# The last F tile of each expert's first product, computed over two halves of 256 slots

## The chip, the cores and the metric

The kernel runs on one core of one Trainium2 chip. The metric is the device time of one execution in microseconds (us), the median of several runs. Three runs of the kernel before gave 821.24, 821.36 and 821.48 us. Less is better.

## The reference

A batch of 4 sequences of 1024 tokens (4096 tokens of width D = 512) passes through two layers, and the input is added at the end:

```
h     = x @ W_cond[category of the sequence] + b_cond[...]         # per sequence
probs = softmax(h @ Wr)                                            # 8 experts
e, p  = argmax(probs), max(probs)
# each expert takes the first 512 tokens that chose it (capacity 4096 / 8)
a     = relu(h[tokens of e] @ W1[e])                               # 512 -> F = 2048
y     = a @ W2[e]                                                  # 2048 -> 512
out   = x;  out[tokens of e] += p * y
```

Everything is float32. The two products of the experts are nearly all of the arithmetic: for each of 8 experts 512 x 512 x 2048 and 512 x 2048 x 512.

## The kernel before

**Three products for one.** Each float32 operand is split into a high part and a low part, both of type fp32r, and a product is the sum of three: high by high, high by low, low by high. `PARTS` on TensorE lists these three pairs. A product over K = 512 is cut in `DK` = 4 blocks of 128, so one output tile of 128 x 512 takes 4 x 3 = 12 matmuls that accumulate in one PSUM bank. Each matmul loads its own 128 x 128 weights first (PEld LDWEIGHTS in the profile), then streams 512 columns through them.

**Stages.** First the conditioned rows h of all 4096 tokens are computed (L968, L972, L984), with the router beside them (L890, L897, L910, L920, L928, L929, L939), and h is stored in DRAM. Then the tokens of the first expert are gathered and transposed (L1036, L1046, L1054). From then on a loop of 4 rounds of two experts each (`par` 0 and 1) does all expert work on TensorE.

**One expert on TensorE.** The first product is made in `FT` = 16 tiles (`j`) of 128 of the F = 2048 hidden units, each over all `CH` = 512 slots of the expert. The weights are a 128 x 128 block of W1, and the moving operand is the transposed tokens `xts`, 512 columns. Tiles 0 and 1 are made by `first_two` (L1092, in an order that follows the arrival of the token blocks), tiles 2 to 15 by the plain loop at L1123 (matmuls at L1133). The tiles go round `AR` = 4 PSUM banks `ffn_ps` (two halves of `acc_ps`, two of `tp_ps`); tile 15 is in the fourth, in `tp_ps`. The second product is made by `second(q)` (L1071, matmuls at L1080) for each quarter q of F: 4 slot blocks x 4 hidden tiles x 3 = 48 matmuls of 512 columns into `y_ps`. Quarter q - 1 follows the last tile of quarter q, so the order at the end of an expert is: tiles 12, 13, 14, 15, then `second(2)` with 48 matmuls, then `second(3)` with 48, then the first two tiles of the next expert. TensorE executes this order as written.

**What follows a tile.** The last matmul of a tile raises `s_acc`. ScalarE then applies Relu and writes the high part into `hts` (L592), VectorE computes the low part (L843) and raises `s_accf`, which frees the bank and lets `second` read the tile: `second(q)` waits for tile 4q + 3 (L1075). Behind each of these two steps the same engines split a piece of the next weights: ScalarE at L525 (W1) or L531 (W2), VectorE at L734 or L740. SyncE loads weights into `stage` (L257, L262), and GpSimd gathers and scatters rows (L421, L428, L460, L467). VectorE scales the outputs at L867.

The waits ahead of tile j at L1127 (weights split), L1129 and L1130 (bank free, that is, tile j - 4 has been read by ScalarE and VectorE) stand in front of its first matmul; the tile's one signal stands on its last.

Of the kernel before, what the change touches and what calls it, by code (L numbers as in the profile page):

```python
# [17 lines left out]
def moe_kernel(nc, x, x_t, cat, cond_w, cond_wt, cond_b, cond_br, w_r, w_1, w_2, out, h_rows):  # L18
# [6 lines left out]
    P = 128  # L25
# [6 lines left out]
    DK = D // P  # L32
    CH = 512
# [5 lines left out]
    FT = F // P  # L39
# [3 lines left out]
    HI, LO = 0, 1  # L43
# [13 lines left out]
    SPLIT_X = [None, None, (3, 4), (6, 7), (12, 14), (16, 17), (21, 22), (22, 24)]  # L57
    SPLIT_W = [None, (4, 4, 5, 5), (11, 11, 12, 13), (16, 17, 18, 19)]
    KEEP_FIRST = 12
    LATE = 4  # L60
    EARLY = TOKENS - LATE * P
    BY_TILE = NT - 2 * TPC
# [11 lines left out]
    with ctx:  # L74
        def sb(name, shape, dt):
            return ctx.enter_context(nc.sbuf_tensor(name, shape, dt))
# [9 lines left out]
        w1s = [sb(f"w1_split{n}", [P, 2, DK, CH], f32r) for n in (1, 0)][::-1]  # L86
        w2s = sb("w2_split", [P, 2, 2, DK, CH], f32r)
        with nc.sbuf_tensor("xt_first", [P, 2, DK, CH], f32), \
                nc.sbuf_tensor("late_parts", [P, 3, LATE, D], bf16) as late_parts:
            pass  # L90
        xts = sb("xt_split", [P, 4, 2, DK, CH], f32r)
# [45 lines left out]
        tok_all = sb("tok_all", [P, E, SB], u32)  # L137
        late_rel = sb("late_rel", [P, LATE], f32)
        window = sb("window", [P, LATE], f32)
        window_at = sb("window_at", [1, LATE], mybir.dt.int32)  # L140
        late_sel = sb("late_sel", [P, LATE, P], bf16)
        put_all = sb("put_all", [P, E, SB], u32)
# [11 lines left out]
        ffn_ps = [acc_ps[:, 0, :], acc_ps[:, 1, :], tp_ps[:, 0, :], tp_ps[:, 1, :]]  # L154
        AR = len(ffn_ps)
# [715 lines left out]
        def _(pe):  # L871
            PARTS = ((HI, HI), (HI, LO), (LO, HI))
# [126 lines left out]
            def keep_warm(times):  # L999

                for _ in range(times):
                    nc.tensor.matmul(acc_ps[:, 1, :], ones[:, :], zeros[:, :], start=True, stop=True)

            pe.wait_ge(s_mask, 1)
            pe.wait_ge(s_zeros, 1)
            keep_warm(KEEP_FIRST)
            pe.wait_ge(s_whalf, 1)
# [61 lines left out]
            with pe.Fori(0, E // 2) as pair:  # L1069
                for par in range(2):  # L1070
                    def second(q):  # L1071
                        pe.wait_ge(s_w2lo, pair * (4 * QN) + 2 * (par * QN + q + 1))
                        if q == 0:
                            pe.wait_ge(s_y, pair * (2 * SB) + par * SB + 1)
                        pe.wait_ge(s_accf, NT + pair * (2 * FT) + par * FT + QF * (q + 1))  # L1075
                        for s in range(SB):
                            for jj in range(QF):
                                j = q * QF + jj
                                for a, w in PARTS:
                                    last = nc.tensor.matmul(y_ps[:, s, :], hts[:, j % HB, a, s * P:(s + 1) * P],  # L1080
                                                            w2s[:, q % 2, w, jj, :],
                                                            start=(j == 0 and (a, w) == (HI, HI)),
                                                            stop=(j == FT - 1 and (a, w) == (LO, HI)))
                            if q == QN - 1:
                                last.then_inc(s_f2, 1)

                    def first_two():

                        x_of = pair * (2 * DK) + par * DK

                        def product(j, k, w, a, start=False, stop=False):
                            return nc.tensor.matmul(ffn_ps[j], w1s[0][:, w, k, j * P:(j + 1) * P],  # L1092
                                                    xts[:, par, a, k, :], start=start, stop=stop)

                        def with_high(k):
                            pe.wait_ge(s_xehi, x_of + k + 1)
                            product(0, k, HI, HI, start=(k == 0))
                            product(0, k, LO, HI)

                        def with_low(k):  # L1100
                            pe.wait_ge(s_xelo, x_of + k + 1)
                            return product(0, k, HI, LO, stop=(k == DK - 1))

                        pe.wait_ge(s_w1lo, pair * (4 * QN) + 2 * par * QN + 2)
                        pe.wait_ge(s_accf, NT + pair * (2 * FT) + par * FT + 2 - AR)
                        with_high(0)
                        product(1, 0, HI, HI, start=True)
                        with_high(1)
                        with_low(0)
                        with_high(2)  # L1110
                        with_low(1)
                        with_high(3)
                        with_low(2)
                        product(1, 0, LO, HI)
                        with_low(3).then_inc(s_acc, 1)
                        product(1, 0, HI, LO)
                        for k in range(1, DK):
                            for w, a in PARTS:
                                last = product(1, k, w, a, stop=(k == DK - 1 and (w, a) == (LO, HI)))
                        last.then_inc(s_acc, 1)  # L1120

                    first_two()
                    for j in range(2, FT):  # L1123
                        slot, jj = (j // QF) % 2, j % QF
                        tile = pair * (2 * FT) + par * FT + j
                        if jj == 0:
                            pe.wait_ge(s_w1lo, pair * (4 * QN) + 2 * (par * QN + j // QF + 1))  # L1127
                        if j == 2 and par == 0:
                            pe.wait_ge(s_quart, 1)  # L1129
                        pe.wait_ge(s_accf, NT + tile + 1 - AR)  # L1130
                        for k in range(DK):
                            for w, a in PARTS:
                                last = nc.tensor.matmul(ffn_ps[j % AR], w1s[slot][:, w, k, jj * P:(jj + 1) * P],  # L1133
                                                        xts[:, par, a, k, :],
                                                        start=(k == 0 and (w, a) == (HI, HI)),
                                                        stop=(k == DK - 1 and (w, a) == (LO, HI)))
                        last.then_inc(s_acc, 1)
                        if jj == QF - 1 and j // QF >= 1:
                            second(j // QF - 1)
                    second(QN - 1)  # L1140
# [34 lines left out]
```

## Time and profile before

| | |
|---|---|
| median of 3 runs | 821.36 us (821.24 to 821.48) |
| span of the profiled execution, first to last instruction | 819.6 us |
| PE busy | 812.9 us, 99%, 4103 matmuls |
| PEld busy | 668.0 us, 82%, 4103 weight loads |
| DVE, ACT, POOL busy | 410.4, 257.3, 241.2 us (50%, 31%, 29%) |
| mean granted TensorE clock | 1.000 |

The profile gives the profiled execution's own time as its span alone. The median of the runs is 1.76 us above that span. PE and PEld are two rows of the same engine: the matmuls, and the loading of their weights, which can run beside a matmul. A matmul's own duration is a latency from start to modelled end, so matmuls that follow each other overlap in the list; the time that one costs in a row of many is the step from one start to the next, which a row with a count gives: (busy - duration of one) / (count - 1), or busy / count in a chain.

### The profile page before, as it was taken

How to read it: one execution, taken by the hardware profiler on the slowest of the kernel's cores; microseconds unless marked ns; L12 is line 12 of the kernel's file. 1: busy time of each engine (PE TensorE's matmuls, PEld its weight loads, DVE VectorE, ACT ScalarE, POOL GpSimd, SP SyncE). 2: the span in 40 equal slices, each digit the busy share in tenths (PEclk: the TensorE clock that was granted, in tenths of full speed). 3: DMA queues.
4: the chain of work that ended last, by engine and by line, in shares of the span. 5: the costliest groups of instructions: out<-in, count | busy, mean ns of one | idle time of the engine just before them, and what ended most of it. 6: DMA issues, size and time to landing. Idle time of an engine off the chain costs nothing.

```text
span 819.6 us, 10809 instructions
## 1 busy us (share of the span) xinstructions
PE 812.9 (99%) x4103; PEld 668.0 (82%) x4103; DVE 410.4 (50%) x575; ACT 257.3 (31%) x350; POOL 241.2 (29%) x240
## 2 busy tenths in 40 slices
PE   9999999999999999999999999999999999999997
PEld 6778788888888888888888888888888888888886
DVE  5678877442644355533653174426443555336531
ACT  3322245330433133332433053304331333324330
POOL 1000127264304540273007320643045401030201
PEclk9999999999999999999999999999999999999999
DMA  8988454543443337341633344444533372216101
GB/s 286 362 293 289 186 174 150 211 141 142 155 179 128 129 103 256 115 139 58 211 122 126 142 154 154 141 141 159 174 128 128 98 256 102 102 59 210 50 0 51
DMA packets 61098, 127.14 MB, mean 155 GB/s; under 512 B 8310, under 2 KB 8310, under 8 KB 60562
## 3 DMA queue, kind: packets, MB, share of 16 engines
q1 hardware_dynamic: 47714, 95.19, 32.6%
q0 software_dynamic: 13216, 31.38, 11.8%
q8 instruction: 14, 0.23, 0.1%
q10 hardware_dynamic: 144, 0.26, 0.1%
q14 instruction: 10, 0.08, 0.0%
HBM read 110.13 MB, written 25.17 MB: 165 GB/s over the span
## 4 chain that ended last, share of the span: by engine, by line
PE 97%; DMA 1%; DVE 0%; SPq 0%; issue 0%; ACT 0%; POOL 0%; POOLq 0%
PE y_ps L1080 42%; PE tp_ps L1133 21%; PE acc_ps L1133 16%; PE acc_ps L984 6%; PE acc_ps L1092 5%; PE tp_ps L984 3%; DMA stage<-x_t 1%; PE tp_ps L910 1%; PE y_ps L890 0%; PE y_ps L939 0%; DVE xt_split L619 0%; PE y_ps L1036 0%; PE y_ps L1054 0%; SPq L281 0%; PE y_ps L920 0%
## 5 line engine op out<-in xcount | busy, mean ns | idle before, releaser
L1080 PE MATMUL y_ps<-w_split,xt_split 128*128 128x512 f32 x1536 | 352.1, 389 | 0.0
L1080 PEld LDWEIGHTS y_ps<-w_split,xt_split 128*128 128x128 f32 x1536 | 288.3, 188 | 59.9
L428 POOL DMA_INDIRECT rows<-h_rows,idx_all x112 | 117.2, 1047 | 240.3 <-DVE turned L833 198.8
L1133 PE MATMUL tp_ps<-xt_split,w_split 128*128 128x512 f32 x768 | 179.3, 389 | 0.0
L1133 PEld LDWEIGHTS tp_ps<-xt_split,w_split 128*128 128x128 f32 x768 | 144.2, 188 | 29.9
L592 ACT ACTIVATE xt_split<-acc_ps 128x512 fp32r<-128x512 f32 x64 | 38.3, 598 | 333.7 <-PE acc_ps L1092 171.6
L1133 PE MATMUL acc_ps<-xt_split,w_split 128*128 128x512 f32 x576 | 134.5, 389 | 0.0
L1133 PEld LDWEIGHTS acc_ps<-xt_split,w_split 128*128 128x128 f32 x576 | 108.1, 188 | 22.5
L843 DVE SCALAR_TENSOR_TENSOR xt_split<-acc_ps,xt_split 128x512 fp32r<-128x512 f32 x64 | 44.3, 692 | 162.7 <-ACT xt_split L592 161.8
L867 DVE SCALAR_TENSOR_TENSOR rows<-y_ps,p_cur,rows 128x512 f32<-128x512 f32 x32 | 24.0, 751 | 133.0 <-PE y_ps L1080 133.0
L734 DVE TENSOR_TENSOR w_split<-stage,w_split 128x1024 fp32r<-128x1024 f32 x66 | 81.0, 1227 | 16.3 <-ACT w_split L525 16.3
L740 DVE TENSOR_TENSOR w_split<-stage,w_split 128x1024 fp32r<-128x1024 f32 x64 | 78.5, 1227 | 16.4 <-ACT w_split L531 16.4
L467 POOL DMA_INDIRECT out<-rows,put_all x32 | 31.4, 981 | 154.3 <-DVE rows L867 154.3
L525 ACT ACTIVATE w_split<-stage 128x1024 fp32r<-128x1024 f32 x66 | 69.4, 1052 | 0.0
L531 ACT ACTIVATE w_split<-stage 128x1024 fp32r<-128x1024 f32 x64 | 67.3, 1052 | 0.0
L592 ACT ACTIVATE xt_split<-tp_ps 128x512 fp32r<-128x512 f32 x64 | 38.3, 598 | 75.1 <-PE tp_ps L1133 75.1
L843 DVE SCALAR_TENSOR_TENSOR xt_split<-tp_ps,xt_split 128x512 fp32r<-128x512 f32 x64 | 44.3, 692 | 34.9 <-ACT xt_split L592 34.9
L984 PE MATMUL acc_ps<-w_split,xt_split 128*128 128x512 f32 x228 | 55.1, 394 | 0.4 <-DVE rows L648 0.4
L421 POOL DMA_INDIRECT rows<-x,tok_all x32 | 44.9, 1403 | 31.3 <-DMA out<-rows,put_all 18.3
L984 PEld LDWEIGHTS acc_ps<-w_split,xt_split 128*128 128x128 f32 x228 | 42.2, 188 | 9.6 <-issue 1.1
L460 POOL DMA_INDIRECT out<-b_rows,drop_all x32 | 32.8, 1024 | 52.9 <-DMA b_rows<-x 43.7
L1092 PE MATMUL acc_ps<-xt_split,w_split 128*128 128x512 f32 x192 | 45.0, 390 | 0.1
(140 smaller groups left out, 381.9 us busy)
## 6 DMA issues: line engine op xcount, KB each, us to landing
stage<-w SPq DMA_DIRECT2D x64, 1024.0 KB, 6.5
b_rows<-x SPq DMA_DIRECT2D x8, 1024.0 KB, 7.7
h_rows<-rows POOLq DMA_DIRECT2D x6, 1024.0 KB, 9.8
stage<-cond_wt SPq DMA_DIRECT2D x4, 1024.0 KB, 9.8
x_more<-x_t SPq DMA_DIRECT2D x4, 1024.0 KB, 9.5
stage<-x_t SPq DMA_DIRECT2D x3, 1024.0 KB, 8.0
stage<-cond_w SPq DMA_DIRECT2D x3, 1024.0 KB, 9.6
h_rows<-rows SPq DMA_DIRECT2D x8, 256.0 KB, 2.5
```

Of the source, the lines that this page charges most:

```text
L421: pool.indirect_dma_start(out=rows[:, 1, s, :], out_offset=None, in_=x, in_offset=bass.IndirectOffsetOnAxis(ap=tok_all[:, e, s:s + 1], axi ...
L428: pool.indirect_dma_start(out=h_quart[:, t * P:(t + 1) * P], out_offset=None, in_=h_parts, in_offset=bass.IndirectOffsetOnAxis(ap=idx_all[ ...
L525: nc.scalar.activation(w1s[slot][:, HI, ks, :], stage[:, slot, ks, :], ACTF.Copy).then_inc(s_w1hi, 1)
L531: nc.scalar.activation(w2s[:, slot, HI, ks, :], stage[:, 2 + slot, ks, :], ACTF.Copy).then_inc(s_w2hi, 1)
L592: nc.scalar.activation(hts[:, j % HB, HI, :], ffn_ps[j % AR], ACTF.Relu).then_inc(s_hhi, 1)
L734: nc.vector.tensor_tensor(w1s[slot][:, LO, ks, :], stage[:, slot, ks, :], w1s[slot][:, HI, ks, :].bitcast(f32), ALU.subtract).then_inc(s_w ...
L740: nc.vector.tensor_tensor(w2s[:, slot, LO, ks, :], stage[:, 2 + slot, ks, :], w2s[:, slot, HI, ks, :].bitcast(f32), ALU.subtract).then_inc ...
L843: nc.vector.scalar_tensor_tensor(hts[:, j % HB, LO, :], ffn_ps[j % AR], 0.0, hts[:, j % HB, HI, :].bitcast(f32), ALU.max, ALU.subtract).th ...
L984: last = nc.tensor.matmul(cond_bank(n), xts[:, c % 4, a, k, t * P:(t + 1) * P], w2s[:, (c // CPB) % 2, w, k, :], start=(k == 0 and (a, w) ...
L1080: last = nc.tensor.matmul(y_ps[:, s, :], hts[:, j % HB, a, s * P:(s + 1) * P], w2s[:, q % 2, w, jj, :], start=(j == 0 and (a, w) == (HI, HI)),
L1092: return nc.tensor.matmul(ffn_ps[j], w1s[0][:, w, k, j * P:(j + 1) * P], xts[:, par, a, k, :], start=start, stop=stop)
L1133: last = nc.tensor.matmul(ffn_ps[j % AR], w1s[slot][:, w, k, jj * P:(jj + 1) * P], xts[:, par, a, k, :], start=(k == 0 and (w, a) == (HI, ...
```

## The change

The last of the 16 tiles of the first product, j = `FT` - 1 = 15, is computed in two passes: the 12 matmuls over slots 0 to 255, then the 12 over slots 256 to 511. Each pass goes through the same 12 blocks of weights, so each block is loaded twice, and each matmul streams 256 columns in place of 512. Both passes write halves of the same PSUM bank. The signal `s_acc` stands on the last matmul of the second pass, the waits ahead of the tile and all other engines' code are as before. Tiles 0 to 14 and the second product are unchanged.

```diff
+    HALVES = (slice(0, CH // 2), slice(CH // 2, CH))
...
                         pe.wait_ge(s_accf, NT + tile + 1 - AR)
-                        for k in range(DK):
-                            for w, a in PARTS:
-                                last = nc.tensor.matmul(ffn_ps[j % AR], w1s[slot][:, w, k, jj * P:(jj + 1) * P],
-                                                        xts[:, par, a, k, :],
-                                                        start=(k == 0 and (w, a) == (HI, HI)),
-                                                        stop=(k == DK - 1 and (w, a) == (LO, HI)))
+                        for cols in HALVES if j == FT - 1 else (slice(0, CH),):
+                            for k in range(DK):
+                                for w, a in PARTS:
+                                    last = nc.tensor.matmul(ffn_ps[j % AR][:, cols],
+                                                            w1s[slot][:, w, k, jj * P:(jj + 1) * P],
+                                                            xts[:, par, a, k, cols],
+                                                            start=(k == 0 and (w, a) == (HI, HI)),
+                                                            stop=(k == DK - 1 and (w, a) == (LO, HI)))
                         last.then_inc(s_acc, 1)
```

## Rows read from the trace of the kernel before

**Rows 1.** The page: span; busy us, share and count of each engine; granted clock in tenths.
```profile
span 819.6 us, 10809 instructions
PE 812.9 (99%) x4103; PEld 668.0 (82%) x4103; DVE 410.4 (50%) x575; ACT 257.3 (31%) x350; POOL 241.2 (29%) x240
...
PEclk9999999999999999999999999999999999999999
```
**Rows 2.** The page: the chain that ended last, share by engine and by line.
```profile
PE 97%; DMA 1%; DVE 0%; SPq 0%; issue 0%; ACT 0%; POOL 0%; POOLq 0%
PE y_ps L1080 42%; PE tp_ps L1133 21%; PE acc_ps L1133 16%; PE acc_ps L984 6%; PE acc_ps L1092 5%; PE tp_ps L984 3%; DMA stage<-x_t 1%; PE tp_ps L910 1%; PE y_ps L890 0%; PE y_ps L939 0%; DVE xt_split L619 0%; PE y_ps L1036 0%; PE y_ps L1054 0%; SPq L281 0%; PE y_ps L920 0%
```
**Rows 3.** The chain in order of time, first expert: start us, us, piece, count.
```profile
172.99 5.44 PE acc_ps L1133 x24
178.43 5.44 PE tp_ps L1133 x24
183.87 21.76 PE y_ps L1080 x96
205.63 5.44 PE acc_ps L1092 x24
```
**Rows 4.** Stretches of about one expert: us, busy us (count) by engine, PEclk, DMA share, GB/s.
```profile
206.00:293.00 87.00, 87.00 (x386) 72.03 (x385) 40.23 (x46) 27.26 (x36) 30.24 (x28) 1.00 0.42 145
...
728.00:815.00 87.00, 86.91 (x384) 71.63 (x382) 40.21 (x46) 27.27 (x36) 14.34 (x12) 1.00 0.21 75
```
**Rows 5.** Timeline at the end of the first expert: start us, us, engine, line, count.
```profile
183.71 12.63 PE L1080 MATMUL y_ps<-w_split,xt_split 128*128 128x512 f32 x55
...
183.91 0.60 ACT L592 ACTIVATE xt_split<-tp_ps 128x512 fp32r<-128x512 f32 x1 [1.17 <-PE tp_ps L1133]
...
184.54 0.69 DVE L843 SCALAR_TENSOR_TENSOR xt_split<-tp_ps,xt_split 128x512 fp32r<-128x512 f32 x1 [0.55 <-ACT xt_split L592]
```
**Rows 6.** Groups of the page: line, shapes, count, busy us, mean ns, idle before.
```profile
L1133 PE MATMUL tp_ps<-xt_split,w_split 128*128 128x512 f32 x768 | 179.3, 389 | 0.0
L1133 PEld LDWEIGHTS tp_ps<-xt_split,w_split 128*128 128x128 f32 x768 | 144.2, 188 | 29.9
```
**Rows 7.** Timeline of PE, f32 transposes of 128 columns, two overlapping windows.
```profile
114.55 1.06 PE L1054 MATMUL y_ps<-ident,x_more 128*128 128x128 f32 x7
114.55 1.18 PE L1054 MATMUL y_ps<-ident,x_more 128*128 128x128 f32 x8
```
**Rows 8.** Timeline of PE, f32 with 32-column weights, two overlapping windows and stretches.
```profile
45.79 1.95 PE L910 MATMUL tp_ps<-x_more,m 128*32 128x128 f32 x64
45.79 1.85 PE L910 MATMUL tp_ps<-x_more,m 128*32 128x128 f32 x60
```
**Rows 9.** Timeline of PE, bf16 matmuls of 128 columns.
```profile
113.18 1.31 PE L1036 MATMUL y_ps<-late_sel,late_parts 128*128 128x128 bf16 x20
```
**Rows 10.** Timeline of the weight loads (PEld) in the first stage, around a pause.
```profile
6.69 0.19 PEld L968 LDWEIGHTS tp_ps<-w_split,xt_split 128*128 128x128 f32 x1
6.92 0.19 PEld L968 LDWEIGHTS y_ps<-w_split,xt_split 128*128 128x128 f32 x1
...
9.50 0.30 PEld L968 LDWEIGHTS acc_ps<-w_split,xt_split 128*128 128x128 f32 x2 [0.58 <-issue]
```
**Rows 11.** Timeline of the matmuls (PE) over the same stretch.
```profile
6.92 0.39 PE L968 MATMUL tp_ps<-w_split,xt_split 128*128 128x512 f32 x1
7.14 0.39 PE L968 MATMUL y_ps<-w_split,xt_split 128*128 128x512 f32 x1
...
9.53 0.70 PE L968 MATMUL acc_ps<-w_split,xt_split 128*128 128x512 f32 x2 [0.18 <-ACT w_split L499]
10.07 0.39 PE L968 MATMUL tp_ps<-w_split,xt_split 128*128 128x512 f32 x1
```
**Rows 12.** The page: DMA queues that carry instructions: packets, MB, share.
```profile
q8 instruction: 14, 0.23, 0.1%
...
q14 instruction: 10, 0.08, 0.0%
```

## The prediction

> **What bounds the kernel now.** I read the page first. TensorE's matmuls fill 812.9 of 819.6 us, every slice of the span shows nine tenths or more of the clock, and no other engine is over 50% busy [rows 1]. The chain that ended last is TensorE for 97%, with one hundredth for the first load of x; L1080, L1133 and L1092, the expert loop, make 84% [rows 2]. Then I read the chain in order of time. Its pieces in the expert loop have no gap: 24 matmuls take 5.44 us and 96 take 21.76 us, 226.7 ns each, one piece starting where the last ends [rows 3]. The table by stages says the same for each later expert: PE busy for 87.00 of 87.00 us and 384 to 386 matmuls, at a granted clock of 1.00 [rows 4]. So TensorE never waits from its first expert to its last, and a matmul added there, or a nanosecond added to one, is paid in full. Nor is there an idle moment for the change to win back.
>
> **What the change does not touch.** Its signal stands on the tile's last matmul, as before, so ScalarE and VectorE get the whole tile at once, and only as much later as the tile takes longer. What they do with it has room. Tile 15 ends at 183.87; Relu starts at 183.91 and the low part ends at 184.54 + 0.69 = 185.23 [rows 3, 5]. The first reader, the second half of the 96 matmuls, starts after 48 of them, at 183.87 + 10.88 = 194.75 [rows 3]. That is 9.5 us of room. A tile that is later by a fraction of a us moves these two engines, and the weight splits behind them, by the same fraction while TensorE is late by it too. So ScalarE, VectorE, SyncE's weight loads, GpSimd's gathers and every wait are worth 0, and what hides them is the 10.88 us of the third quarter's second product. That is also why nothing can be won by an earlier start: nobody waits for this tile. If the cover were gone, the tile's 1.3 us of Relu and low part would stand on the path, 8 times 1.3 = 10 us; nothing in the change takes it away. One wait stands ahead of tile 15, for the bank (L1130), and the matmuls run past it without a gap [rows 3]; the change adds none.
>
> **What it costs, step by step.** Removed: 12 matmuls of 512 columns per expert, 12 x 226.7 = 2720 ns. Added: 24 of 256 columns, each with its own weight load of the same size. The trace has no fp32r matmul of 256 columns, so its step s must be bounded. The break-even is 2720 / 24 = 113.3 ns; each ns of s over it costs 24 x 8 = 192 ns.
>
> Term one, the stream. In 226.7 ns at the full 2.4 GHz level, 512 columns take 213.3 ns at one column per clock, which leaves 13.3 ns beside them. Half the columns take 106.7 ns. If the 13.3 ns are paid once per matmul whatever its length, s = 120.0. The nearest row with weights of 128 columns in f32, the transposes of 128 columns, has one more matmul for 0.12 us (1.18 less 1.06) [rows 7]. Those are shorter than 256 columns and take as long, so they don't run at a column per clock; plain f32 with weights of 32 columns shows 0.10 us for four more that run side by side [rows 8], which is 128 columns at half pace. Their 0.12 us is then 106.7 + 13 to 15: a stretch of streaming as long as the new one, and about the same extra. The bf16 matmuls of 128 columns step by (1.31 - 0.22) / 19 = 57 ns [rows 9], 53.3 and a little. They show that pairs of load and matmul can be issued at least twice as fast as needed, so issue costs 0.
>
> Term two, the weight load. Its length of 188 ns [rows 6] is longer than 120, and is the reason to look closely. But it is a latency. After a pause two loads come together: two take 0.30 us, so the second starts 0.30 - 0.19 = 0.11 us after the first [rows 10]. One load thus holds its path for 0.11 us. And a load starts with the matmul ahead of it: the load for y_ps at 6.92, where the matmul for tp_ps starts at 6.92, and the matmul for y_ps at 7.14 [rows 10, 11]. So a load of about 110 ns lies beside a stream of 120 ns and is hidden, by 10 ns only. Today it is hidden by over 100. When it isn't hidden, as behind the pause, the first matmul of the pair takes 0.70 - 0.39 = 0.31 us in place of 0.23 [rows 11].
>
> The bounds of s: below, 109 ns, a stream of 106.7 with bf16's small extra, or the load's 0.11 us alone. Above, 227 ns, where a half-length matmul costs what a full one does (both mechanisms are among the rivals). I take 120.5, between the 120.0 of the half stream and the 0.12 us of rows 7 with its rounding. Per expert 24 x 120.5 - 2720 = +172 ns, for 8 experts +1.4 us. The stages ahead of the experts and the scatter behind are unchanged. The span goes from 819.6 to 821.0. The median of the runs stands 1.76 us over the span, an offset that the change doesn't touch, so the time is 821.36 + 1.4 = 822.7 us.
>
> The granted clock is 1.00 in each stretch [rows 4], its 2.4 GHz level, and TensorE stays without a pause, so I take it unchanged. Memory traffic is unchanged too.
>
> The Trainium skill, "TensorE: Matmul & The Clock Gate", section "Back-to-back issue gap", gives 262 cycles for 256 columns and 518 for 512. An estimate from that page alone is 24 x 109.2 - 12 x 215.8 = +30 ns per expert, +0.2 us in all. The trace disagrees at 512, where it shows 226.7 ns, so I don't use its extra.
>
> **The rivals.**
>
> A. The load becomes the pace. If a load starts with the matmul ahead, holds its path for 110 ns, and the 13.3 ns are a handover that is paid behind whichever ends last, s = 3 + 110 + 13 = 126 ns. That is +304 ns per expert, +2.4 us: 823.8. For it: the margin is only 10 ns, and the trace never shows a load this long under a stream this short. Against it: the 0.31 us of the first matmul behind the pause [rows 11] holds at most one load and one full step (0.11 + 0.23 = 0.34), with no second handover. It decides from s = 122 on.
>
> B. A short matmul gains nothing. Either a load isn't started until its neighbour is over, which puts 0.11 us beside each 120, or a short f32 stream falls to the half pace of rows 7 and 8, 213 + 13. Both give s = 227: 12 more full steps, +2.72 us per expert, +21.8 us: 843.1. If only the 188-ns latency were exposed, s = 191, +1.86 us per expert and +14.9 in all: 836.3. For it: 128 columns of f32 do go at half pace. Against it: fp32r at 512 goes at full pace, and rows 10 and 11 show load and matmul starting together.
>
> The Trainium skill has the first of these as a rule: the same page, "Part 3: Packing small matmuls", says that a weight load overlaps a matmul in flight only when its row group is another. All loads here use all 128 rows, and yet the load at 6.92 runs inside the matmul that starts at 6.92 [rows 10, 11]: the trace disagrees.
>
> C. Not slower. The 13.3 ns may belong to a long stream, or grow with its columns (one in sixteen). Then 256 columns take 106.7 + 3 to 7 ns and the load's 110 ns becomes the floor: s = 110, 24 x 110 - 2720 = -80 ns, -0.6 us in all: 820.7, at s = 113 no change. It decides below the break-even of 113.3. For it: bf16 shows 3 ns beside 128 columns [rows 9]. Against it: the f32 transposes pay 13 or more beside a stream of 107.
>
> D. The longer code. The loop's body gets 24 more matmuls and 24 more loads, consumed twice as fast for 2.9 us. Instructions come by DMA, 24 packets in the span, 0.31 MB [rows 12]. If a fetch at one tile came late by 0.5 us in each expert, +4 us on top: 826.7. Against it: no gap today at any tile or turn of the loop [rows 3, 4].
>
> That the change doesn't do what it says is ruled out by its form: the two passes load different blocks in turn, so no load can be shared or merged.
>
> **How the numbers follow.** Runs of this kernel differ by 0.24 us; I take 0.2%, 1.6 us, as what can be told from no change. The forecast, s from 119.5 to 122, is 822.5 to 823.0 and has 0.64. A has 0.20, B 0.06 (0.02 of it the exposed load), C 0.06, D 0.04. No change within 1.6 us reaches to s = 121.8, which takes nearly all of the forecast, and most of C: 0.60 + 0.04 = 0.64. Slower: A, B, D and the edge of the forecast, 0.34. Faster needs s under 105, below the stream itself: 0.02. The range leaves out B, most of D, and the lower half of C: 821.3 to 825.0. Its upper end is s = 132, A with some ns more at each change of weights.
>
> **What would show it.** In the changed profile PE should count 4103 + 96 = 4199 matmuls and as many loads. A group at L1133's new line with 128x256 and count 192 should stand there, its own duration about 389 - 107 = 282 ns. The chain in order of time should show the last tile as 24 matmuls in 2.89 us (2.72 before), and each expert 0.17 us longer than its 87.04. Loads should start 120 ns apart in the tile. If they are 126 apart it is A, at 227 B, at 110 C; a gap before a matmul that nothing releases would be D. ScalarE's and VectorE's busy times should stay, and no wait of TensorE should appear in front of the fourth quarter's second product. An unchanged tile with a changed step elsewhere would make the whole reasoning wrong.

## The result, and the profile after

The changed kernel takes 822.56 us, the kernel before beside it 821.21 us (20 runs each). The ratio is 1.0016 with a 95% interval of 1.0010 to 1.0023: +1.35 us, under the 0.2% that I called telling, though twenty runs do tell it from nothing. One run of each twenty is far off, 904.75 us before and 1376.13 us after at a granted clock of 0.557, and the ratio leaves these two out. The forecast was 822.7 us, +1.4. The span of the profiled execution went from 819.6 to 821.0 us, as forecast; that execution took 822.73 us.

The page after, with the lines that answer to [rows 1] and [rows 2]:

```profile
span 821.0 us, 11001 instructions
PE 814.6 (99%) x4199; PEld 673.4 (82%) x4199; DVE 410.6 (50%) x575; ACT 257.3 (31%) x350; POOL 241.8 (29%) x240
...
PE 97%; DMA 1%; DVE 0%; SPq 0%; issue 0%; ACT 0%; POOL 0%; POOLq 0%
```

There are 4199 matmuls, 96 more, PE is busy for 1.7 us more, and ScalarE and VectorE are as busy as before. The chain that ended last, in order of time (start us, us, piece, count), answers to [rows 3]:

```profile
173.01 5.44 PE acc_ps L1135 x24
178.45 5.59 PE tp_ps L1135 x36
184.04 21.79 PE y_ps L1081 x96
205.83 5.44 PE acc_ps L1093 x24
...
293.05 5.44 PE acc_ps L1093 x24
```

The piece with tiles 14 and 15 now has 12 + 24 matmuls and takes 5.59 us in place of 5.44, the second product behind it 21.79 in place of 21.76. One expert takes 293.05 - 205.83 = 87.22 us, which was 292.67 - 205.63 = 87.04 before, where 205.63 stands in [rows 3] and the chain goes on with this line:

```profile
292.67 5.44 PE acc_ps L1092 x24
```

That is +0.18 us, eight times, which is the whole difference of the spans. The groups by shape, and the timeline of the short tile in two windows that differ by one matmul:

```profile
L1135 PE MATMUL tp_ps<-xt_split,w_split 128*128 128x512 f32 x672 | 157.5, 389 | 0.0
...
L1135 PE MATMUL tp_ps<-xt_split,w_split 128*128 128x256 f32 x192 | 24.3, 283 | 0.0
```
```profile
181.01 2.56 PE L1135 MATMUL tp_ps<-xt_split,w_split 128*128 128x256 f32 x20
181.01 2.67 PE L1135 MATMUL tp_ps<-xt_split,w_split 128*128 128x256 f32 x21
```

A matmul's own duration fell from 389 to 283 ns, by 106 ns, about the 106.7 that 256 columns take at one column per clock. One more costs 0.11 to 0.12 us; by the starts in the trace nearly all steps from one short matmul to the next are 120 ns, and the first of each row is 113 or 114. The loads start 120 ns apart too. What follows the tile, to be held against [rows 5]:

```profile
184.08 0.60 ACT L593 ACTIVATE xt_split<-tp_ps 128x512 fp32r<-128x512 f32 x1 [1.33 <-PE tp_ps L1135]
...
184.71 0.69 DVE L844 SCALAR_TENSOR_TENSOR xt_split<-tp_ps,xt_split 128x512 fp32r<-128x512 f32 x1 [0.70 <-ACT xt_split L593]
```

Both start 0.17 us later than before, and TensorE has no wait in the expert loop.

### The profile page after: what moved, and what is told of

Its sections match the earlier page's. It is cut to its first block, busy times and chain, and to the rows that moved or that the text cites. A ratio compares the mean times of both kernels' runs of the same rounds, so it can differ in the third digit from the quotient of the medians.

```text
span 821.0 us, 11001 instructions
## 1 busy us (share of the span) xinstructions
PE 814.6 (99%) x4199; PEld 673.4 (82%) x4199; DVE 410.6 (50%) x575; ACT 257.3 (31%) x350; POOL 241.8 (29%) x240
## 4 chain that ended last, share of the span: by engine, by line
PE 97%; DMA 1%; DVE 0%; SPq 0%; issue 0%; ACT 0%; POOL 0%; POOLq 0%
PE y_ps L1081 42%; PE tp_ps L1135 21%; PE acc_ps L1135 16%; PE acc_ps L985 6%; PE acc_ps L1093 5%; PE tp_ps L985 3%; DMA stage<-x_t 1%; PE tp_ps L911 1%; PE y_ps L891 0%; PE y_ps L940 0%; DVE xt_split L620 0%; PE y_ps L1055 0%; PE y_ps L1037 0%; SPq L282 0%; SPq L281 0%
## 5 line engine op out<-in xcount | busy, mean ns | idle before, releaser
L1135 PE MATMUL tp_ps<-xt_split,w_split 128*128 128x512 f32 (+1 forms) x864 | 180.5, 365 | 0.0
L1135 PEld LDWEIGHTS tp_ps<-xt_split,w_split 128*128 128x128 f32 x864 | 150.2, 189 | 26.8
```

The lines of the kernel that those rows point to most:

```text
L1135: last = nc.tensor.matmul(ffn_ps[j % AR][:, cols], w1s[slot][:, w, k, jj * P:(jj + 1) * P], xts[:, par, a, k, cols], start=(k == 0 and (w, ...
```

## The experiments

In each, the edit is to the changed kernel unless it says otherwise. They ran in three groups, each group with the kernel before on the same chip. For the first group (e1 to e4) that kernel itself took 834 to 857 us, and the traces of e1 to e4 have pauses of TensorE in or behind tile 15 that nothing releases and that no other trace has. So of those four only the steps inside the tile are read, and the four were run again as e9 to e12.

**The step at other widths: four passes over 128 slots.**

```diff
-    HALVES = (slice(0, CH // 2), slice(CH // 2, CH))
+    HALVES = tuple(slice(n * P, (n + 1) * P) for n in range(TPC))
```

> Tile 15 in four passes over 128 slots, 48 matmuls with 48 loads. Theory (a step is columns / 2.4 plus 13.3 ns, but not shorter than the time a weight load holds its path, 110 to 113 ns as behind the pause): step 110 to 113, the tile takes 5.3 to 5.4 us in place of 2.72, +20.5 to +21.6 us over before, about 842.4. If there were no such floor: step 66.7, tile 3.2 us, +3.8 us, 825.0. Rival A (the load sets the 120 ns of the halves) and the half-pace rival (128 columns take 106.7 + 13.3 ns): step 120, tile 5.76 us, +24.3 us, 845.5.

Steps of 110 to 114 ns outside the pauses; time 874.2 us against 847.8, not usable.

> Tile 15 in four passes over 128 slots once more; in the first run the kernel before itself took 834 to 857 us, so only the steps could be read: 110 to 114 ns, and 42 instruction packets in place of 14, with pauses in two experts. Theory (floor of 112 ns by the load's path): tile 5.38 us, +21.2 us over before; and where the longer loop body has to be fetched again in each round, up to 1 us more: 842.5 to 843.5. If the pauses of the first run belong to the longer code, they come again and it is over 850.

843.14 us against 821.23: +21.9 us, ratio 1.0266 (1.0249 to 1.0283). The chain at the end of one expert:

```profile
267.75 8.03 PE tp_ps L1135 x60
275.78 21.87 PE y_ps L1081 x96
```

The 12 long ones take 2.72, so the 48 short ones take 5.31, 111 ns each, and 0.11 us more shows behind them: 5.42 - 2.72 = +2.70 us, +21.6 in eight experts. The time is 0.3 us over that, and 0.40 us stand at one turn of the loop (below). With a stream of 53.3 + 13.3 ns alone it would have been +3.8. So there is a floor under short matmuls, and it is the weight load's path. By the starts in the trace the loads of the tile stand 111 or 112 ns apart, as two loads did behind a pause in [rows 10] (0.11 us), and the matmuls aren't what holds them: the second short matmul of each tile starts 57 or 58 ns after the first. (No run narrowed the weights at this length.) The floor is 112 ns and not 120, so the load doesn't set the step of the halves, and rival A falls. Half pace falls as well, for these fp32r operands: 120 was expected, and 57 ns is too short for it. The pauses of the first run did not return.

**320 and 192 slots.**

```diff
-    HALVES = (slice(0, CH // 2), slice(CH // 2, CH))
+    HALVES = (slice(0, 320), slice(320, CH))
```

> Tile 15 in two passes over 320 and 192 slots. Theory: steps of 133.3 + 13.3 = 146.7 ns and, since 80 + 13.3 = 93.3 is under the floor, 110 to 113; per expert 12 x (146.7 + 112) - 2720 = +384 ns, +3.1 us over before. Rival A (load sets 120): +480 ns per expert, +3.8 us. Half pace below 256 columns: 12 x (146.7 + 173.3) - 2720 = +1120 ns, +9.0 us. Without a floor it would cost the same as two halves, +1.3 us.

Steps of mostly 146 to 147 ns for 320 columns, 109 to 117 for 192 (the first of a row 88 to 90); time 853.6 against 847.8.

> Two passes over 320 and 192 slots once more. By the steps of the first run (146.7 and 112 ns, 36 matmuls in 5.79 us) the tile takes 3.07 us, +0.35 us per expert and some hundredths behind it: +2.8 to +3.1 us over before. Rival A would have 120 for the short step and +3.8.

824.31 us against 821.23: +3.1 us, ratio 1.0036 (1.0024 to 1.0049).

```profile
266.10 5.79 PE tp_ps L1135 x36
271.89 21.81 PE y_ps L1081 x96
```

The tile takes 3.07 us. The long step is 320 / 2.4 + 13.3, to the nanosecond in most of the row. The short one would be 93.3 by that rule; its loads start 111 or 112 ns apart, and behind the first step of 88 to 90 it keeps their pace. So the same 512 slots cost 1.7 us more in all when they are cut where one part goes under the floor: the halves lie just above it.

**Weights of 32 columns.** Of tile 15 only 32 of the 128 hidden units are computed.

```diff
+                        width = G if j == FT - 1 else P
...
-                                    last = nc.tensor.matmul(ffn_ps[j % AR][:, cols],
-                                                            w1s[slot][:, w, k, jj * P:(jj + 1) * P],
+                                    last = nc.tensor.matmul(ffn_ps[j % AR][:width, cols],
+                                                            w1s[slot][:, w, k, jj * P:jj * P + width],
```

> The halves of the change, but the weights of tile 15 are only 32 columns wide (96 of the tile's 128 hidden units are not computed): the load is a quarter as long, the stream the same 256 columns. If the 13.3 ns belong to the f32 stream itself: step 120, +1.4 us over before, as the change. If they belong to the loading of 128 columns of f32 weights, or if the load sets the step (rival A): step 107 to 109, 24 x 108 - 2720 = -128 ns per expert, -1.0 us.

Steps of 117 to 119 ns; time 848.2 against 847.8.

> Halves with weights of 32 columns once more (96 of the tile's 128 hidden units are left out). By the steps of the first run (117 to 118 ns, 36 matmuls in 5.55 us): +0.13 us per expert, +1.1 us over before, where the change has +1.4: nearly all of the 13.3 ns stay with a load a quarter as long, so they belong to the stream of f32 columns. If the load made them: -1.0 us.

822.28 us against 821.23: +1.05 us, ratio 1.0012 (1.0002 to 1.0022). The groups by shape:

```profile
L1136 PE MATMUL tp_ps<-xt_split,w_split 128*32 128x256 f32 x192 | 23.9, 280 | 0.0
L1136 PEld LDWEIGHTS tp_ps<-xt_split,w_split 128*32 128x32 f32 x192 | 20.7, 108 | 3.0
```

The load's latency fell from 188 to 108 ns, which is 80 ns for 96 columns. The step fell by 2. So the load is hidden, and the extra 13.3 ns are not the price of loading: 11 of them stay. (The difference of the times, 1.05 against the change's 1.35, is within their intervals; the reading rests on the steps.)

**bf16 operands.** Constants in place of the tile's data; its result is left out.

```diff
+                                    if j == FT - 1:
+                                        weights, moving = ones[:, :], zeros[:, cols]
...
```

> The 24 matmuls of tile 15 with bf16 operands of the same shapes (constants, so this tile's result is left out of the sum). The bf16 matmuls of 128 columns stepped by 56 to 57 ns, 53.3 and 3. Theory (the 13.3 ns come with f32 operands): step 109, 24 x 109 - 2720 = -104 ns per expert, -0.8 us against before. If every matmul of 256 columns costs 120 whatever its type: +1.4 us.

Steps of 109 to 110 ns, the first of a row 120; time 855.4 against 847.8.

> Halves with bf16 operands for tile 15 once more (constants, the tile's result is left out). By the steps of the first run (109 ns, 36 matmuls in 5.36 us): -0.08 us per expert, -0.4 to -0.8 us against before. If a matmul of 256 columns costs 120 whatever its type: +1.4.

820.37 us against 821.23: -0.86 us, ratio 0.9991 (0.9981 to 1.0000).

```profile
264.82 5.35 PE tp_ps L1139 x36
270.18 21.78 PE y_ps L1081 x96
```

24 matmuls in 5.35 - 2.72 = 2.63 us, 109.6 ns each: 106.7 and 3. With the step under the break-even of 113.3 the cut tile is shorter than the whole f32 one, as the prediction's arithmetic has it. That is read from the chain, 0.07 us in each expert; the interval of the ratio touches 1. The 13.3 ns come with the f32 type of the operands. The values, constants here, don't explain it: the bf16 matmuls of [rows 9] work on real data and have the same 3 ns. Both operands were changed at once, so which of them brings the 13.3, and by what, stays open; e11 speaks against the loading of the weights.

**The two passes turned inside out.**

```diff
-                        for cols in HALVES if j == FT - 1 else (slice(0, CH),):
-                            for k in range(DK):
-                                for w, a in PARTS:
+                        halves = HALVES if j == FT - 1 else (slice(0, CH),)
+                        for k in range(DK):
+                            for w, a in PARTS:
+                                for cols in halves:
...
```

> The change with its two passes turned inside out: each block of weights is loaded twice in turn, for slots 0 to 255 and then for 256 to 511. Theory: 24 loads and 24 steps of 120.0 all the same, +1.4 us over before, equal to the change. Rival: a load of the weights that are already there is left out or is shorter, and a step falls towards 109: 12 x 109 + 12 x 120 - 2720 = +28 ns per expert, +0.2 us.

822.36 us against 821.27: +1.1 us, ratio 1.0014 (1.0004 to 1.0023). Steps of 120 ns; the tile's piece in the chain is again 36 matmuls in 5.59 us, the group the same as the change's:

```profile
L1136 PE MATMUL tp_ps<-xt_split,w_split 128*128 128x256 f32 x192 | 24.3, 283 | 0.0
```

All 4199 loads are in the trace. A load of weights that are already there is neither left out nor shorter, at least not so that the step shows it. The order is worth nothing.

**Every tile of the plain loop in halves.**

```diff
-                        for cols in HALVES if j == FT - 1 else (slice(0, CH),):
+                        for cols in HALVES:
```

> Tiles 2 to 15 of every expert in halves (14 in place of one). Theory (120.0 ns a step, and the next product's first two matmuls later by 16 ns in all behind each row of short ones, three rows of halves that end in the second product or four with the row ahead of it): 14 x 160 + 4 x 10 = 2.28 us per expert, +17.9 to +18.4 us over before, 839.3. Rival D (issue or fetching of code falls behind in a longer row of short matmuls, 48 and 96 of them): steps over 120 later in a row, or gaps, and more than +20 us.

840.52 us against 821.27: +19.25 us, ratio 1.0235 (1.0218 to 1.0252). The chain of one expert, from its first tiles to its end:

```profile
208.29 5.44 PE acc_ps L1093 x24
213.73 5.75 PE tp_ps L1135 x48
219.48 5.76 PE acc_ps L1135 x48
225.24 5.76 PE tp_ps L1135 x48
231.00 10.91 PE y_ps L1081 x48
...
275.84 21.79 PE y_ps L1081 x96
297.63 0.17 issue
297.80 5.75 PE acc_ps L1093 x24
...
476.78 5.59 PE acc_ps L1093 x24
...
655.61 5.65 PE acc_ps L1093 x24
```

48 short matmuls in 5.76 us are 120.0 ns each, however long the row, so issue keeps up. One expert takes 297.63 - 208.29 = 89.34 us, +2.30, and eight give +18.4. That alone is the top of what I expected (17.9 to 18.4), and the time is 0.85 us over it. The spans differ by 839.1 - 819.6 = 19.5 us. Of the 1.1 us that this leaves, 0.34 lie ahead of the experts, whose first starts at 118.61 us here and at 118.27 in the kernel before. The rest stands at the three turns of the loop. The first 24 matmuls of a round, all of 512 columns, take 5.75, 5.59 and 5.65 us where they take 5.44 otherwise, and at the first turn 0.17 us of waiting comes on top: 0.84 us together. So something of rival D is there. The DMA queue that carries instructions shows it, in this kernel:

```profile
q8 instruction: 50, 0.82, 0.4%
```

and in e9:

```profile
q8 instruction: 42, 0.69, 0.3%
```

It was 14 packets before [rows 12] and 14 after. In the trace of before, the last packet of this queue starts at 268 us, ahead of the end of the first round of the loop, while in these two kernels they go on in every round, two of them within some 3 us of each turn. So the longer body is fetched anew each time. In e9 the first two turns cost nothing, and the third costs 0.12 us of waiting and 0.28 us in the matmuls behind it:

```profile
656.61 0.12 issue
656.73 5.72 PE acc_ps L1093 x24
```

That these costs are late fetches is argued from where they stand; no run separates it.

**The cover taken away.** The third quarter's second product goes ahead of tile 15; first in the kernel before.

```diff
+                        if j == FT - 1:
+                            second(QN - 2)
                         pe.wait_ge(s_accf, NT + tile + 1 - AR)
...
-                        if jj == QF - 1 and j // QF >= 1:
+                        if jj == QF - 1 and 1 <= j // QF < QN - 1:
```

> The kernel before with the third quarter's second product moved ahead of tile 15, so that the fourth quarter's stands directly behind it. My text put the price of the lost cover at the tile's Relu and low part, 1.3 us, +10 us in all. Rival: the fourth quarter also waits for the W2 split that the same engines do behind these (ScalarE L531, VectorE L740, which ended at 186.72 where tile 15 ended at 183.87), 2.85 us, +22.8 us in all.

858.6 us against 821.27: +37.3 us, ratio 1.0460 (1.0442 to 1.0477). Neither number holds. The chain behind tile 15:

```profile
194.68 1.06 ACT w_split L531
195.73 0.02 issue
195.76 1.24 DVE w_split L740
196.99 0.12 issue
197.12 12.79 PE y_ps L1080 x48
```

The waits of TensorE (us in total, times, longest), and the stretches around one of them (us, PE busy and count, granted clock, DMA share, GB/s):

```profile
PE y_ps L1080 <- DVE w_split L740: 23.7, 8, 3.0
```
```profile
194.00:197.00 3.00, 0.15 (x1) 1.00 0.02 3
197.00:201.00 4.00, 3.88 (x10) 0.58 0.69 191
201.00:205.00 4.00, 4.00 (x19) 0.99 0.91 343
```

The same piece of the chain in the sixth expert, and its granted clock over the 4 us behind the pause:

```profile
656.71 11.17 PE y_ps L1080 x48
```
```profile
656.70:660.70 4.00, 3.99 (x18) 1.00 0.58 214
```

The wait is for the W2 split, as the rival said: 2.97 us eight times, 23.7 us. On top, the 48 matmuls behind it take 12.79 us in place of 10.88, and that has two parts. In the sixth expert the pause is as long, the granted clock stays at 1.00, and they take 11.17: 0.29 us go with the pause alone. In the seven others the granted clock is 0.58 over the first 4 us, that is mostly at the 1.2 GHz level, and 12.79 - 11.17 = 1.62 us more go with the clock. 23.7 + 8 x 0.29 + 7 x 1.62 = 37.4, which is the result. Why the clock held in one expert, no run shows.

> The same with tile 15 in halves. Theory (the signal comes with the last matmul, so halves are pure cost): 1.3 to 1.4 us more than the same order with the whole tile. Rival (without cover the halves win something back): equal to it or faster.

859.86 us, 38.6 over before and 1.26 over e7, with the same waits:

```profile
PE y_ps L1081 <- DVE w_split L741: 23.7, 8, 3.0
```

Halves are pure cost without the cover too. No experiment points to an f32 version that is faster than the kernel before, so none was run.

## Why the prediction was right

- **TensorE is the path, with no idle moment.** Shown: the chain after is the chain before with one piece of 5.59 for 5.44 and one of 21.79 for 21.76.
- **The step of 120.5 ns.** It is 120.0: 106.7 of stream and 13.3 fixed. That the 13.3 are paid per matmul whatever its length is shown at 320, 256 and 512 columns, in a row of its like; that they belong to f32 operands and hardly to the load, by e12 and e11. The half ns I added from [rows 7] was not there (24 x 8 x 0.5 = 0.1 us).
- **A support that was none.** I took the 0.12 us of the plain f32 transposes [rows 7] as "a stretch of streaming as long as the new one, and about the same extra". By the starts in the trace they step by 121 ns, while e9's matmuls of the same shape with fp32r operands step by 111 and can stand 58 apart. So the two types don't go at the same pace, the transposes are no measure of this step, and that they gave 120 as well is luck. The half stream with its 13.3 ns carried the forecast alone.
- **A term that I left out.** The second product behind the tile takes 0.03 us more: by the starts in the trace its first four steps are 234, 235, 229 and 232 ns in place of 226.7. The first short step is 7 ns less. Both and the right step make 0.18 us per expert where I had 0.172; the agreement to 0.1 us is partly these cancelling.
- **The load's path of 110 ns under the stream.** Shown by e9 and e10: the floor is 112 ns. A (0.20) was given too much. Its handover of 13 ns behind the load doesn't exist, for at the floor the step is the load's alone.
- **B and half pace** are out by e9 and e10; **C** is what bf16 does, not f32. **D** did not come with 96 more pairs of load and matmul in the span; with longer bodies something of it shows, 0.84 us in e5 and 0.40 in e9.
- **The cover.** Its claim that the other engines cost 0 held. The room of 9.5 us was right for the low part, but the same product also waits for the W2 split queued behind it on the same engines, which ended at 186.72: for that the room is 194.75 - 186.72 = 8.0 us. The price I named if the cover were gone, 10 us, was wrong for this reason: I followed the tile's own chain and forgot the split, and the clock. It is 37 us.

## What to carry to other kernels

Where TensorE is the path without a gap, cutting a tile's columns is priced nearly by the step alone: here columns / 2.4 + 13.3 ns for fp32r operands at a granted clock of 1.00 (measured at 256, 320 and 512 columns), and in a row not under the 112 ns that its 128-column weight loads stand apart. Cut it only if somebody waits for the first part, and keep each part above the floor. When you price a cover, list everything the next consumer waits for, and add what a pause of that length does to the clock.

## What was not expected of the hardware

- The extra of 13.3 ns per f32 matmul: 3 ns in bf16 at the same shape, 11 with weights of 32 columns.
- A pause of 2.97 us cost 0.29 us more behind it in one expert, where the clock held, and 1.91 in the seven others, 1.62 of it with the clock.
- A loop that is fetched anew in every round, 42 or 50 instruction packets in the span in place of 14, still cost only 0.40 and 0.84 us.
- An fp32r matmul of 128 columns can be followed by the next after 58 ns; in a row its weight loads keep it at 111.
- In the first group TensorE has waits of up to 1.7 us between two matmuls, in tile 15 or within some 12 us behind it, in some experts, with nothing that releases them. The fetching of code hardly makes them: e2 has them at 544 to 555 us, while the last packet of its queue q8 starts at 274 and none of q14 between 529 and 747. Why they come stays open; nothing here was run on it.
